# Attention with eight PSUM banks shared out as four and two instead of three and three

## The reference

```
x   [8, 512, 256]   ctx [8, 512, 192]   16 heads of width 16
q = layernorm(x) @ Wq + bq;  k = ctx @ Wk + bk;  v = ctx @ Wv + bv
a = softmax(clip(q k^T / 4, -10000, 10000))      per head, 512 x 512
x = x + tanh(g0) * ((a v) @ Wo + bo)
x = x + tanh(g1) * (sum over 8 experts of gate_e * ffn_e(layernorm(x)))
```

## Time and profile before

| | |
|---|---|
| time, median of 3 (lowest, highest) | 1924.23 us (1922.54, 1926.05) |
| time of the profiled execution | 1925.5 us |
| its span | 1923.7 us |
| TensorE busy in the span | 1870.8 us, 97% |
| VectorE, ScalarE busy | 1294.5 us, 1280.5 us (67% each) |
| attention, from the first plain score to the last turned one | 92 to 543 us of the span |
| one batch in the middle of attention | 54.6 us |

### The profile page before, as it was taken

How to read it: one execution, slowest core, us unless ns; L and a number is a source line. 1 busy time by engine, 2 the same in 40 slices (tenths; PEclk the granted TensorE clock), 3 DMA queues, 4 the chain that set the end, 5 groups by cost and what they waited for, 6 DMA issues and landing times.

```text
span 1923.7 us, 25738 instructions
## 1 busy us (share of the span) xinstructions
PE 1870.8 (97%) x8868; PEld 1342.3 (70%) x8868; DVE 1294.5 (67%) x2279; ACT 1280.5 (67%) x2145; POOL 146.4 (8%) x327
## 2 busy tenths in 40 slices
PE   7999999999999999999999999999999999999998
PEld 6733333343367887888788788888878888887886
DVE  6788888888757666556665655665565576556555
ACT  4447777777765556766676766767677676767665
POOL 6201011101124500000000000000000000000000
PEclk9979999999999999999999999999999999999999
DMA  8932332222212353233322323333232433322321
GB/s 288 365 79 81 83 86 73 80 80 73 70 45 89 150 206 118 88 120 142 127 107 96 110 88 132 142 116 115 88 110 88 146 132 115 112 88 88 112 107 57
DMA packets 97245, 220.84 MB, mean 115 GB/s; under 512 B 31314, under 2 KB 49492, under 8 KB 87892
## 3 DMA queue, kind: packets, MB, share of 16 engines
q1 hardware_dynamic: 97108, 219.12, 33.0%
HBM read 178.57 MB, written 40.24 MB: 114 GB/s over the span
## 4 chain that ended last, share of the span: by engine, by line
PE 83%; DVE 7%; ACT 3%; issue 2%; POOL 0%; DVEq 0%; ACTq 0%; POOLq 0%
PE ps_y L2167 32%; PE ps_h L2114 28%; PE ps_t L834 5%; PE ps_h L2087 5%; PE ps_y L2099 4%; PE ps_o L845 4%; DVE low L981 3%; PE ps_m L870 1%; ACT probs_T L1158 1%; PE ps_s L823 1%; DVE attn L1004 1%; PE ps_m L856 1%; DVE x_res L1014 1%; DVE x_lo L1065 1%; DVE xn_b L1057 1%
## 5 line engine op out<-in xcount | busy, mean ns | idle before, releaser
L2467 DVE TENSOR_TENSOR h_lo<-gelu,h_hi 128x512 fp32r<-128x512 f32 x512 | 353.0, 694 | 437.0 <-ACT h_hi L2367 405.7
L2114 PE MATMUL ps_h<-x_hi,w_pair 128*128 128x512 f32 x1568 | 562.7, 393 | 1.8 <-ACT gelu L2364 1.0
L2364 ACT ACTIVATE gelu<-early,b 128x512 f32<-128x512 f32 x336 | 243.3, 724 | 229.6 <-DVE early L2616 221.0
L2114 PEld LDWEIGHTS ps_h<-x_hi,w_pair 128*128 128x128 f32 x1568 | 294.4, 188 | 78.1 <-issue 6.1
L981 DVE TENSOR_REDUCE low<-ps_s 128x1 f32<-128x512 f32 x512 | 321.4, 682 | 31.9 <-PE ps_s L823 29.5
L2367 ACT ACTIVATE h_hi<-gelu 128x512 fp32r<-128x512 f32 x448 | 283.5, 633 | 41.9 <-ACT gelu L2364 1.1
L2114 PE MATMUL ps_h<-x_lo,w_pair 128*128 128x512 f32 x784 | 309.4, 395 | 0.0
L1158 ACT ACTIVATE probs_T<-ps_t 128x512 f32<-128x512 f32 x384 | 207.8, 600 | 94.0 <-PE ps_t L834 92.2
L2616 DVE TENSOR_TENSOR early<-ps_h,copy 128x512 f32<-128x512 f32 x336 | 230.6, 686 | 49.3 <-PE ps_h L2114 49.3
L823 PE MATMUL ps_s<-k_st,q_st 48*128 48x512 f32 x512 | 205.6, 479 | 3.1 <-SPq L727 2.0
L2167 PE MATMUL ps_y<-h_hi,w_lo 128*128 128x512 f32 x512 | 202.7, 396 | 0.0
(11 more groups left out here) (263 smaller groups left out, 2532.4 us busy)
## 6 DMA issues: line engine op xcount, KB each, us to landing
x_hi<-blocks_scratch SPq DMA_DIRECT2D x28, 1024.0 KB, 5.1
x_lo<-blocks_scratch SPq DMA_DIRECT2D x28, 1024.0 KB, 8.8
x_hi<-blocks_scratch SPq DMA_DIRECT2D x28, 768.0 KB, 6.7
x_lo<-blocks_scratch SPq DMA_DIRECT2D x28, 768.0 KB, 10.2
gate<-gates_scratch SPq DMA_DIRECT2D x64, 256.0 KB, 3.2
q_st<-q_scratch SPq DMA_DIRECT2D x192, 64.0 KB, 2.3
k_st<-k_scratch SPq DMA_DIRECT2D x192, 64.0 KB, 2.3
k_scratch<-k_hl SPq DMA_DIRECT2D x8, 1024.0 KB, 5.5
```

The costliest lines, as they stand in the source:

```text
L2114: mm = pe.matmul(bank, w[wp], x[xp], start=start and n == 0, stop=n == 2, skip_group_check=not start)
L2364: act.activation(gelu[:, c % GELUS, :], src, ACT.Gelu_apprx_tanh, bias=b1[p][:, j:j + 1]).then_inc(gelu_done, 1)
L2467: dve.tensor_tensor(h_lo[:, j % RING, :], gelu[:, j % GELUS, :], h_hi[:, j % RING, :].bitcast(F32), ALU.subtract).then_inc(h_ready, 1)
```

## The change

The eight banks are shared out anew: `ps_s` gets four, `ps_t` two; `ps_o` and `ps_m` keep one each. The bank of a product is now its number modulo 4 or 2. S number n waits for the minimum of S number n-4, T number n for the exponential of T number n-2. The one-column product that sums the flags at the end of attention moves from the third `ps_t` bank to the second. The order of the instructions on every engine, their number and their shapes are the same.

```diff
-BANKS = 3
+SCORE_BANKS = 4
+TURNED_BANKS = 2
...
-def bank_of(turn, at):
-
-    return (turn + at) % BANKS
+def score_bank(b, at):
+
+    return (b * PRODUCTS + at) % SCORE_BANKS
+
+
+def turned_bank(b, at):
+
+    return (b * PRODUCTS + at) % TURNED_BANKS
...
-    ps_s = [n_.ps(f"ps_s{i}", [P, SEQ]) for i in range(BANKS)]
-    ps_t = [n_.ps(f"ps_t{i}", [P, SEQ]) for i in range(BANKS)]
+    ps_s = [n_.ps(f"ps_s{i}", [P, SEQ]) for i in range(SCORE_BANKS)]
+    ps_t = [n_.ps(f"ps_t{i}", [P, SEQ]) for i in range(TURNED_BANKS)]
...
-    def free_after(b, at):
+    def free_after(b, at, banks):
 
-        return b * PRODUCTS + at - BANKS + 1
+        return b * PRODUCTS + at - banks + 1
...
-            wait(pe, low_done, free_after(b, at))
-            pe.matmul(ps_s[bank_of(turn, at)][:], q_st[g][rows, j // 2, t * P:(t + 1) * P], k_st[g][rows, j // 2, :],
+            wait(pe, low_done, free_after(b, at, SCORE_BANKS))
+            pe.matmul(ps_s[score_bank(b, at)][:], q_st[g][rows, j // 2, t * P:(t + 1) * P], k_st[g][rows, j // 2, :],
...
-            wait(pe, exp_done, free_after(b, at))
+            wait(pe, exp_done, free_after(b, at, TURNED_BANKS))
...
-            pe.matmul(ps_t[BANKS - 1][:, 0:1], ones[:], fits_sum[:], start=True, stop=True).then_inc(fits_in_psum, 1)
+            pe.matmul(ps_t[TURNED_BANKS - 1][:, 0:1], ones[:], fits_sum[:], start=True, stop=True).then_inc(fits_in_psum, 1)
```

More of the change, by code:

```diff
@@ L831, in scores_T @@
                 pe.wait_ge(rows_sent, group_no(b, g) * 32 + 32)
-            wait(pe, exp_done, free_after(b, at))
+            wait(pe, exp_done, free_after(b, at, TURNED_BANKS))
             rows = half_rows(j, ROWS + 1)
-            pe.matmul(ps_t[bank_of(turn, at)][:], k_st[g][rows, j // 2, k * P:(k + 1) * P], q_st[g][rows, j // 2, :],
+            pe.matmul(ps_t[turned_bank(b, at)][:], k_st[g][rows, j // 2, k * P:(k + 1) * P], q_st[g][rows, j // 2, :],
                       start=True, stop=True).then_inc(t_in_psum, 1)
@@ L980, in lows @@
                 column = (j % 2) * 2 * TT + (j // 2) * TT + t
-                dve.tensor_reduce(low[:, g % 2, column:column + 1], ps_s[bank_of(turn, at)][:], AX_X, ALU.min).then_inc(low_done, 1)
+                dve.tensor_reduce(low[:, g % 2, column:column + 1], ps_s[score_bank(b, at)][:], AX_X, ALU.min).then_inc(low_done, 1)
         def check_lows(b, g):
@@ L1082, in set_flag @@
             dve.wait_ge(fits_in_psum, 1)
-            dve.tensor_scalar(keep["clip_flag"][:], ps_t[BANKS - 1][:, 0:1], 3 * HEADS * TOKENS - 0.5, None, ALU.is_lt).then_inc(fits_summed, 1)
+            dve.tensor_scalar(keep["clip_flag"][:], ps_t[TURNED_BANKS - 1][:, 0:1], 3 * HEADS * TOKENS - 0.5, None, ALU.is_lt).then_inc(fits_summed, 1)
         take = {"out": normalise, "y": add_residual, "xnT": split, "pick": keep_logits}
@@ L1157, in exps @@
                 act.wait_ge(t_in_psum, n * GROUP + i + 1)
-                act.activation(probs_T[k][:, TURNED_HEADS[i], :], ps_t[bank_of(turn, (g * TT + k) * GROUP + i)][:], ACT.Exp, scale=-1.0).then_inc(exp_done, 1)
+                act.activation(probs_T[k][:, TURNED_HEADS[i], :], ps_t[turned_bank(b, (g * TT + k) * GROUP + i)][:], ACT.Exp, scale=-1.0).then_inc(exp_done, 1)
         def copy_out(b, g):
```

## The result

| | before | changed |
|---|---|---|
| median (lowest, highest) | 1924.0 us (1922.54, 1926.05) | 1945.64 us (1941.76, 1946.08) |
| ratio, 95% interval | | 1.0106 [1.0094, 1.0118] |
| span of the profiled execution | 1923.7 us | 1944.2 us |
| weight load of the first and the last turned product | 111.7, 542.4 us | 111.6, 562.0 us |

By the medians the changed kernel is 21.6 us slower where 12.0 were forecast; the two profiled executions differ by 20.5. The last turned product is 19.6 us late, so nearly all of it is lost inside attention.

The account below looks back on a forecast made before the run. Attention's coupled TensorE, VectorE and ScalarE, none full, were taken to set the pace, with turned products waiting for exponentials. Batch 0's 4.0, middle batches' 6.2 and batch 7's 1.8 made 12.0 us: 1936 us, range 1929 to 1947.

Parts of the forecast that it names:

- more than the sum: Rival, 16%: in attention T0's wait delays scores, VectorE starves, credit and cover fail; 21 us more, 1946.
- the cover by VectorE: Middle batches after (1,3): VectorE's unbroken work covers TensorE's payments in (2,0), (2,1), (2,2), 0.46 us together.
- The price of a step: Attention steps: each pays 0.47 us less its gap (`probs_v`'s delay behind the exponentials today), nothing where that is wider.
- The gain of the fourth score bank: Step (1,3): S1 no longer held, `probs_v` 0.47 us earlier, of which VectorE can gain 0.24.
- Batches 0 and 7: First and last attention batch: they pay 4.0 and 1.8 us for the waits.
- The clock falls: Rival, 3%: one batch falls back to TensorE's lower clock, 16 steps x 1.46 = 23 us, 1960.
- A granted clock under 1.00 after 124 us: Sign in the changed profile that would show the prediction wrong; no size given.

Follow-up runs that it names:

- run 1: Kernel before, three and three banks, with only the turned product's wait made one product stricter: 1942.5 us, ratio 1.0103.
- run 6: Changed kernel with extra unread products beside the turned ones in the last two groups of the last batch: 1937.25 us, ratio 1.0074.
- run 7: Kernel before, fed at the end as in run 5, plus one unread same-shape product beside each of the 32 first plain scores: 1922.97 us, ratio 0.9998.
- run 9: Kernel before, three and three banks, with the turned product's wait two products stricter: 2444.56 us, one execution.
- run 5: Kernel before with extra unread products beside the turned ones in the last two groups of the last batch: 1923.06 us, ratio 0.9995.
- run 2: Changed kernel with the pools swapped, two score banks and four turned ones: 1974.48 us, ratio 1.0256.
- run 8: Kernel before with `probs_v` of the step before moved behind T2 and S2: 1947.23 us, ratio 1.0115.

## Why the prediction came out as it did

The direction, the range and the mechanism of the waits held, and the sum of them nearly to the number: 12.0 us forecast, 11.7 measured. The total did not: 21.6 us. The median lies where the rival "more than the sum" put it (1946), but by another cause than that rival's: the steps that had slack still pay nothing, and the cover by VectorE came. That the total still fell into the range is luck: the range's upper end came from that rival, and nothing in it stood for the clock.

*The price of a step* was right to a few hundredths. Steps with a gap of 0.12 pay 0.33 to 0.37, those with 0.28 to 0.30 pay 0.19 (0.17 forecast), (3,3) pays 0.43 (0.42), (0,2), (1,0), (1,2) and (3,2) pay nothing; `probs_v` stands 0.48 behind the pair (0.47). Run 1 shows that it is the wait and nothing else.

*The gain of the fourth score bank* was right: step (1,3) gives 0.41 (0.47), run 1 lacks it.

*The cover by VectorE* was right, and a little more than forecast: a middle batch pays 0.89 to 1.04 us where 1.03 were forecast, the six some 5.8 in place of 6.2. (2,1) pays 0.10 and not 0.26, and (2,3) and (3,0) give back 0.15 and 0.06.

*Batches 0 and 7* were right. They have to be counted from T2 to T2, since a T0 itself stands 0.9 us later behind the T2 before it than it did (1.25 in place of 0.34), which counted from T0 would go to batch 0 and be missing in batch 7. By runs 6 and 7, and less 0.1 for the clock, batch 0 pays 4.2 (4.0 forecast) and batch 7 1.75 (1.8). In batch 7 (2,1) pays 0.15 and not 0.35, and (3,0) gives 0.2 back.

So the waits come to 4.2 + 5.8 + 1.75 = 11.7 us, 12.0 forecast.

*The step that failed* is the rival "The clock falls". I priced it at 3% and as a whole middle batch at the lower clock, with the argument that batch 2 kept its clock through 3 us of idle; and the sum had no term for it. What happened is shorter spells. In the profiled execution the rise in batch 0 came 4.1 us later, a spell of 3.4 us came in batch 5, and one of 20.5 us where attention ends; the mean clocks of all four executions, 0.984 to 0.986, say that the others had about as much. The last is worth 5.5 us in batch 7 (59.83 against 54.36 when fed) and about 1 net in the experts; batch 5 took 2.12 more than before where its neighbours took 0.95 more: 1.2. The later rise I put at 1.4: 4.1 us in which a step takes 4.17 us in place of 2.71. Together 9.1 us, which with the 11.7 of the waits makes 20.8, where the profiled executions differ by 20.5. A granted clock under 1.00 after 124 us was one of the prediction's own signs of being wrong.

Not all of this is shown to come from the change. That the spell at the end cost its time is shown by runs 5 and 6. That the stricter wait brings such spells is likely, not shown for each: in run 1, with the same wait, the mean clocks go from 0.980 to 0.992, in the kernel before only from 0.990 to 0.993, and in run 9 the lower clock is the rule. What decides how long a spell gets stays open, and so does whether the banks have a part in it. A spell at the start of batch 5 is in all three profiles of the changed kernel, fed or not, and in those of runs 2 and 8; it is in none of the four of the kernel before, fed or not, and not in run 1's. The later rise can't be put to the change: where the first scores are not fed with 128 rows, it comes at 118.1, 121.8 and 123.5 us in the kernel before and at 118.5 and 127.6 in the changed one.

What I should have seen is in the earlier trace rows, where batch 7 has a granted clock of 0.99 and 353 matmuls in 66.80 us against 323 in batch 2's 54.55: the last two groups of batch 7 have no plain scores to run beside the turned ones, so TensorE does less there, and it was there, at the handoff, that the kernel before had its own 3.4 us at the lower clock. Here the change was dearest where TensorE already worked least. The Trainium skill tells of this in "TensorE: Matmul & The Clock Gate", section "A second HAM failure mode: psum-queue depth-cycling": short idles between bank cycles can be enough for the clock to swing. I had set it aside since the trace before showed no swing in the middle; the changed kernel's trace agrees with it, in the spells at 390 and 547 us: in the 10.40 us before the first of them TensorE was busy for 9.12.

No version here beats the kernel before: fed at the end it is the same within what the measurement tells.

## What to carry to other kernels

Before taking a bank from a rotation, ask which later instruction already waits for the release that the shorter rotation would need, and what did its work in that wait's shadow. Here the price of a step is the 0.47 us of one product and its hand-over less the slack behind it, and it could be read off the trace step by step. The other pool's gain counts only where a held instruction is the last thing in the way: one step in 16. And when a change adds waits on TensorE, give the clock a term of its own, priced at the places where TensorE has the least to do, since such spells can cost nearly as much as all the waits, here 9 us beside 11.7.

## What was not expected of the hardware

At the lower clock a turned product takes 0.79 us in place of 0.49 and its weight load 0.28 in place of 0.18, so what the clock takes comes on top of the waits: some 9 us beside 11.7 in the changed kernel. In run 9, whose waits are over 2 us a step longer, 1.2 GHz held for nine tenths of attention.

The same kernel can land on several times, and its mean granted clock goes with them: run 1's executions lie between 1938.21 us (mean clock 0.992) and 1954.73 (0.980).

A product of a plain score's tile (48 rows) and one of 128 rows that take turns are far from free even on idle cycles: 0.74 us for the two at the full clock and 1.23 at the lower one, while a second product on the other half of the rows cost nothing that shows (run 7, first turned product at 111.7 us as before). And 26 more matmuls made the changed kernel 8.4 us faster, by the medians of runs apart (1937.25 against 1945.64).
